# Graph network and mixture-of-experts kernel, one core: x plus normed x made in one ScalarE pass, GpSimd's bias add behind its gathers, x2 turned at the end of the outer layer, normalised rows ahead of the masks

## Chip, cores and metric

The kernel runs on one core of a Trainium2 chip. The metric is the time of one execution in device microseconds, the median of several runs.

## What is computed

6250 nodes with 256 features, 100000 edges with 96 features, sorted by target node. A graph network step comes first, then a mixture of 16 experts with two chosen per node. Both take layer-normalised rows and add their result to the rows they were given.

```python
# node network: edge_attr summed, maximised and averaged over each target node
out1 = segment_sum(edge_attr, col);  out2 = segment_max(edge_attr, col) or 0;  out3 = out1 / max(cnt, 1)
h = concatenate([x, out1, out2, out3, u[batch]], axis=1)
h = relu(h @ W1 + b1) @ W2 + b2
return h + x                                   # x here: the layer-normalised rows

# outer program
x = x + gnn(layernorm(x), ...)                 # so x1 = x + normed x + relu(...) @ W2 + b2
x = x + ffn(layernorm(x))                      # router, two of 16 experts, last layer norm
```

What matters here is x1 = (x + normed x + b2) + g, where g is the node network's output. Its first part, x + normed x + b2, is called RES in the kernel. x2 is the layer-normalised x1; its rows go to memory for the experts and, turned, to the router.

## The kernel before

All five engines are programmed by hand, each in its own block, and each runs its instructions in the order in which its code is written. They meet through counting semaphores.

**Edges.** VectorE scans ten chunks of edges backwards (running sum and running maximum of 96 features, 192 scans a chunk) and SP stores them. This runs until about 570 us, beside the node network.

**Node network.** It takes 25 macro tiles of 250 nodes, two sub-tiles of 125, from 122 to 771 us. Step i does:
- *TensorE* (`gnn_step`, L1088 on): first half of layer 1 (`layer1`, L1034 and L1036, closed by L1038), the router of two steps ago (`router`, L1067), second half of layer 1, the transposes of the next step's inputs (`turn`, L1015 and L1018), then layer 2 (`layer2`, L1048) in two halves, one for each sub-tile. Between these two, `between2` puts the transposes of x2 of the step before (`turn_x2`, L1060). The second half of layer 1 writes banks that ScalarE's first relu must have emptied.
- *ScalarE* (`gnn_step`, L877 on): store of x1, moments of the next x (`moments1`, L791 and L796), its share in the carry of the next macro tile (`carry_in`, L774 to L782), first relu (`relu`, L826), logits (L867), moments of x1 (`moments2`, L835 and L840), load of x two steps ahead (`load_x`, L800), then `mask_rows`: the masked edge results (L806 to L808) and the normalised node rows XN (L812). Then the second relu, `take_turned` (L817 to L819), x2 (`write_x2`, L848) and its store, `take_x2` (L863), and last `take_g` (L874), which copies g out of PSUM.
- *GpSimd* (`rows_step`): `add_rows` (L600), x1 = g + RES; `residual`, the next RES in two adds (L617 XN + x, L619 + b2); `cut` (L578); `norm1` (L591 to L595); `join` (L582 to L586); `norm2` (L605 to L610) of x1; and `gather` two steps ahead: an index copy (L563), a chain of branches on how many chunks must be in memory (L568), and six indirect DMAs (L571 to L573, twice), each issued by GpSimd itself.

`add_rows(i)` waits for g of step i and for RES of step i. Everything on ScalarE behind the store of x1 waits for `add_rows`.

```python
def residual(i, g, b):            # GpSimd
    pool.wait_ge(x1_ready, i)     # the RES before has been read
    pool.wait_ge(xr_got[b], ...); pool.wait_ge(node_rows, i + 1)
    RES = XN[b] + XR[b]           # L617
    RES = RES + b2bc              # L619
```

**Experts.** From 771 us TensorE runs 113 expert tiles (L1144, L1158, L1166) on rows that GpSimd gathers (L658) and scatters (L664). Its first instructions wait for the last-but-one macro tile's logits (L867). A last norm follows.

Of the kernel before, what the change touches and what calls it, by code (L numbers as in the profile page):

```python
# [28 lines left out]
P = 128  # L29
# [68 lines left out]
def after(i, g, b, n=1):  # L98

    return i + n, g + (b + n) // 2, (b + n) % 2  # L100


def gnn_moe_kernel(nc, x, dst, edge_attr, u, gW1, gb1, gW2, gb2, gate_w, gate_b,
# [83 lines left out]
    with ExitStack() as ctx:  # L187
        def sem(name):
            return ctx.enter_context(nc.semaphore(name))
# [32 lines left out]
        rowU = k.take(TILES, parts=NT, dt=U32)  # L222
        mean1, dev_1, rstd_1, nmr_1 = (k.take(2, parts=NT) for _ in range(4))
        Lo = k.take(TILES, NX, parts=NT)
# [144 lines left out]
        xr_got = [sem(f"xr_got{i}") for i in range(2)]  # L369
        residual_ready, x1_ready = sem("residual_ready"), sem("x1_ready")  # L370
        moments2_step, norm2_step, rstd2_ready = sem("moments2_step"), sem("norm2_step"), sem("norm2_rstd_ready")
# [146 lines left out]
        def _(pool):  # L518
# [68 lines left out]

            def norm1(i):
                s2 = Steps(pool, norm1_step, i * 2)
                hold(pool, moments1_step, i * 4 + 4)  # L590
                s2.mark(pool.tensor_scalar(dev_1, dev_1, 1.0 / D, EPS, ALU.mult, ALU.add))  # L591
                s2.wait()
                s2.mark(pool.tensor_tensor(rstd_1, dev_1, rpow, ALU.pow))
                s2.wait()
                pool.tensor_tensor(nmr_1, mean1, rstd_1, ALU.mult).then_inc(rstd1_ready, 1)  # L595

            def add_rows(i):
                pool.wait_ge(g_out, i + 2)
                pool.wait_ge(residual_ready, 2 * i + 2)
                pool.tensor_tensor(GO, GO, RES, ALU.add).then_inc(x1_ready, 1)  # L600
# [10 lines left out]

            def residual(i, g, b):
                if not isinstance(i, int) or i:
                    pool.wait_ge(x1_ready, i)
                pool.wait_ge(xr_got[b], (g + 1) * 16)
                pool.wait_ge(node_rows, i + 1)
                pool.tensor_tensor(RES, XN[b], XR[b][0:NT], ALU.add).then_inc(residual_ready, 1)  # L617
                pool.wait_ge(residual_ready, 2 * i + 1)
                pool.tensor_tensor(RES, RES, b2bc, ALU.add).then_inc(residual_ready, 1)  # L619

            def rows_step(i, g, b):
                more = not isinstance(i, int) or i + 1 < MACROS
                norm = not isinstance(i, int) or i >= 1
                if norm:
                    add_rows(i - 1)
                residual(i, g, b)
                if more:
                    cut(*after(i, g, b))
                    norm1(i + 1)
                    join(*after(i, g, b))  # L630
                if norm:
                    norm2(i - 1)
                if not isinstance(i, int) or i + 2 < MACROS:
                    gather(*after(i, g, b, 2))
            pool.sem_inc(joined, 1)
            gather(0, 0, 0)
            norm1(0)
            cut(0, 0, 0)
# [70 lines left out]
        def _(act):  # L709
# [91 lines left out]

            def mask_rows(i, g, b):
                act.wait_ge(joined, i + 2)
                for a in range(2):
                    j = bass.ds(2 * (MACROS - 1 - i) + a, 1)
                    act.activation(NB[b][:, a, 0:2 * EF], RAW[b][:, a, :, :].rearrange("p s f -> p (s f)"), ACT.Identity, scale=has[:, j])  # L806
                    act.activation(NB[b][:, a, 2 * EF:2 * P], RAW[b][:, a, 0, 0:EF - REST], ACT.Identity, scale=rch[:, j])
                    act.activation(NB[b][:, a, 2 * P:3 * P].rearrange("p (n r) -> p n r", n=QUAD), spread(RAW[b][:, a, 0, EF - REST:EF], 1, QUAD),  # L808
                                   ACT.Identity, scale=rch[:, j])
                act.wait_ge(rstd1_ready, i + 1)  # L810
                for a in range(2):
                    ins = act.activation(XN[b][:, a, :], XR[b][0:NT, a, :], ACT.Identity, bias=nmr_1[:, a:a + 1], scale=rstd_1[:, a:a + 1])  # L812
                ins.then_inc(node_rows, 1)

# [62 lines left out]
            def gnn_step(i, g, b, to=None):  # L877
# [13 lines left out]
                if norm:  # L891
                    moments2(i - 1, 0)
                    moments2(i - 1, 1)
                if not isinstance(i, int) or i + 2 < MACROS:
                    act.wait_ge(residual_ready, 2 * i + 2)
                    load_x(i + 2, b)
                if more:
                    mask_rows(*after(i, g, b))
                relu(i, 1)
                if more:  # L900
                    take_turned(*after(i, g, b))
                if norm:
                    write_x2(i - 1)
                    store_x2(i - 1, to)
                    take_x2(i - 1)
                take_g(i, g, b)
            moments1(0, 0, 0, 0)
# [75 lines left out]
        def _(pe):  # L983
# [104 lines left out]
            def gnn_step(i, g, b, amid1=None, behind1=None, amid2=None):  # L1088
# [5 lines left out]

                def between2():
                    if not isinstance(i, int) or i >= 1:
                        turn_x2(i - 1)
                    if amid2:
                        amid2()
                layer1(i, g, b, between1)  # L1100
                if behind1:
                    behind1()
                if not isinstance(i, int) or i + 1 < MACROS:
                    turn(*after(i, g, b))
                layer2(i, g, b, between2)
            turn(0, 0, 0)
# [522 lines left out]
```

## Time and profile before

| | |
|---|---|
| median of 3 runs | 1328.63 us (1326.2 to 1332.45) |
| the profiled execution: time | 1334.45 us |
| its span | 1332.7 us |
| granted TensorE clock, mean | 0.909 of full speed |
| node network | 122 to 771 us |
| experts | 771 to 1222 us |
| TensorE busy | 1185.9 us (89%) |
| GpSimd busy | 773.3 us (58%) |
| ScalarE busy | 646.1 us (48%) |
| VectorE busy | 788.0 us (59%) |

Times of the profile are microseconds from the span's start. A matmul of 32-bit numbers stands as two records, so a group of 800 is 400 matmuls. `PE` is TensorE, `PEld` its weight load, `DVE` VectorE, `ACT` ScalarE, `POOL` GpSimd; `ACTq` is an instruction of ScalarE's queue that is not counted as busy. In brackets stands how long the engine sat idle before the instruction and what ended it; "issue" is idle time for which the profile shows no releaser. A DMA issued by GpSimd occupies GpSimd for the time that it takes to write its descriptors, and that is what L571 to L573 show.

### The profile page before, as it was taken

To read this page: it belongs to the slowest core of one execution; us is meant where nothing else is said; L and a number is where in the kernel's file an instruction comes from. 1 tells how busy PE (TensorE), PEld (TensorE's weight loads), DVE (VectorE), ACT (ScalarE), POOL (GpSimd) and SP (SyncE) were. 2 spreads that over 40 slices of the span, in tenths; PEclk is the share of its full clock that TensorE was granted. 3 is DMA by queue.
4 is the path that set the end of the run, shared out by engine and by line. 5 is a ranking of instruction groups with operands and counts; after the bars stand their busy time and mean duration, and the time that the engine had idled before them with its cause. 6 is when DMAs were issued, how large, how long until landed. Compare 5 with 4: busy or idle time off the path is not lost.

```text
span 1332.7 us, 28448 instructions
## 1 busy us (share of the span) xinstructions
PE 1185.9 (89%) x6684; PEld 1003.7 (75%) x6685; DVE 788.0 (59%) x3039; ACT 646.1 (48%) x1969; POOL 773.3 (58%) x1061
## 2 busy tenths in 40 slices
PE   2003999999999999999999989999999999999798
PEld 1003888888888888878888888899999999997343
DVE  4999999899799899903534014542222222222886
ACT  5963556655665665655664332223333333333554
POOL 4876666666666667666754235556666666663222
PEclk7555999999999999989999989999999999998555
DMA  9986677768758775592110348856666666664763
GB/s 313 287 269 232 201 275 284 283 237 318 256 215 294 276 239 189 218 334 80 47 45 28 115 155 296 269 174 205 212 212 204 211 212 211 210 212 123 244 203 93
DMA packets 131029, 282.67 MB, mean 212 GB/s; under 512 B 25609, under 2 KB 38283, under 8 KB 130821
## 3 DMA queue, kind: packets, MB, share of 16 engines
q1 hardware_dynamic: 93937, 218.40, 48.3%
q0 software_dynamic: 26048, 43.47, 10.4%
q10 hardware_dynamic: 10964, 19.96, 4.4%
q8 instruction: 23, 0.38, 0.1%
q14 instruction: 57, 0.47, 0.1%
HBM read 167.27 MB, written 114.25 MB: 211 GB/s over the span
## 4 chain that ended last, share of the span: by engine, by line
PE 63%; DMA 10%; issue 9%; POOL 8%; ACT 7%; POOLq 2%; DVE 1%; ACTq 1%; SPq 0%; DVEq 0%
PE ps L1158 14%; PE ps L1166 13%; PE ps L1048 8%; PE ps L1034 7%; PE ps L1036 7%; DMA mem<-piece_carry,mem 4%; PE ps L1199 3%; PE ps L1201 3%; POOL mem L571 2%; POOL mem L572 2%; PE ps L1144 2%; DMA mem<-x_normed,mem 2%; DMA mem<-in_dst_dram,mem 2%; POOL mem L554 2%; ACT mem L728 1%
## 5 line engine op out<-in xcount | busy, mean ns | idle before, releaser
L924 ACT ACTIVATE mem<-ps,mem 128x128 f32<-128x128 f32 x452 | 128.9, 368 | 306.8 <-PE ps L1158 304.8
L1158 PEld LDWEIGHTS ps<-mem 128*128 128x128 f32 x1808 | 221.4, 194 | 7.9 <-issue 3.0
L1158 PE MATMUL ps<-mem 128*128 128x128 f32 x1808 | 223.9, 278 | 1.5 <-issue 1.5
L1034 PE MATMUL ps<-mem 128*128 128x250 f32 x800 | 208.5, 383 | 13.5 <-ACT mem L826 11.9
L1166 PE MATMUL ps<-mem 128*128 x904 | 215.7, 382 | 2.8 <-issue 2.6
L1253 DVE TENSOR_TENSOR_SCAN mem<-ps,mem 128x80 f32<-128x80 f32 x960 | 207.9, 297 | 0.3
L1257 DVE TENSOR_TENSOR_SCAN mem<-ps,mem 128x80 f32<-128x80 f32 x960 | 207.8, 302 | 0.0
L1036 PE MATMUL ps<-mem 128*128 128x250 f32 x800 | 204.4, 378 | 0.0
L664 POOL DMA_INDIRECT expert_rows<-mem x113 | 113.5, 1004 | 126.9 <-DVE mem L1515 112.6
L1048 PE MATMUL ps<-mem 128*125 128x256 f32 x800 | 181.0, 379 | 0.7 <-ACT mem L826 0.7
L1166 PEld LDWEIGHTS ps<-mem 128*128 128x128 f32 x904 | 163.5, 191 | 22.7 <-issue 4.9
L1034 PEld LDWEIGHTS ps<-mem 128*128 128x128 f32 x800 | 152.7, 194 | 33.2 <-ACT mem L826 14.2
L1036 PEld LDWEIGHTS ps<-mem 128*128 128x128 f32 x800 | 153.8, 192 | 18.6
L1048 PEld LDWEIGHTS ps<-mem 128*125 128x125 f32 x800 | 146.3, 188 | 21.1 <-ACT mem L826 1.1
L1508 DVE COPY mem<-ps 128x256 f32<-128x256 f32 x113 | 47.8, 424 | 178.2 <-PE ps L1144 175.9
L1515 DVE TENSOR_TENSOR mem<-ps,mem 128x256 f32<-128x256 f32 x113 | 47.9, 424 | 171.1 <-PE ps L1166 160.3
L658 POOL DMA_INDIRECT mem<-x_normed,mem x113 | 112.7, 998 | 35.4 <-issue 13.0
L1015 PE MATMUL ps<-mem 125*128 125x125 f32 x100 | 20.6, 288 | 90.5 <-ACT mem L812 90.5
L826 ACT ACTIVATE mem<-ps,mem 128x250 f32<-128x250 f32 x200 | 77.0, 467 | 48.6 <-PE ps L1038 48.6
L571 POOL DMA_INDIRECT mem<-run_max,mem x50 | 63.6, 1272 | 46.5 <-issue 46.5
L1015 PEld LDWEIGHTS ps<-mem 125*128 125x128 f32 x100 | 11.6, 145 | 97.7 <-issue 97.7
L554 POOL DMA_INDIRECT mem<-in_dst_dram,mem x50 | 62.1, 1241 | 29.7 <-ACT mem L745 14.7
(252 smaller groups left out, 1696.1 us busy)
## 6 DMA issues: line engine op xcount, KB each, us to landing
mem<-in_L_ffn_w_dram SPq DMA_DIRECT2D x129, 512.0 KB, 9.4
run_sum<-mem SPq DMA_DIRECT2D x80, 480.0 KB
run_max<-mem SPq DMA_DIRECT2D x80, 480.0 KB
mem<-in_edge_attr_dram SPq DMA_DIRECT2D x72, 480.0 KB, 8.0
mem<-expert_rows SPq DMA_DIRECT2D x22, 512.0 KB, 5.4
x_rows<-mem ACTq DMA_DIRECT2D x25, 256.0 KB, 4.0
x_normed<-mem ACTq DMA_DIRECT2D x25, 256.0 KB
mem<-in_x_dram ACTq DMA_DIRECT2D x24, 256.0 KB, 4.1
```

What stands on the lines that cost most here:

```text
L554: pool.indirect_dma_start(out=SR[:, slot % RING, :], out_offset=None, in_=dst2, in_offset=bass.IndirectOffsetOnAxis(rowU[:, j:j + 1], 0)). ...
L571: pool.indirect_dma_start(out=GM[b][:, a, :], out_offset=None, in_=s_max[0:edges], in_offset=last).then_inc(gathered[b], 16)
L658: pool.indirect_dma_start(out=XG[b], out_offset=None, in_=x2_d[0:rows], in_offset=bass.IndirectOffsetOnAxis(slot_now[b], 0)).then_inc(xg_g ...
L664: pool.indirect_dma_start(out=ya_d, out_offset=bass.IndirectOffsetOnAxis(into_now[b], 0), in_=YO[b], in_offset=None).then_inc(yo_stored[b] ...
L924: ins = act.activation(hT[b][:, c, :], bank(2 + b, c * P, (c + 1) * P), ACT.Relu, bias=eb1c[:, bass.ds(e, 1), c])
L1034: pe.matmul(h, W1x[:, c, hc * P:(hc + 1) * P], XT[b][:, c, :], start=(c == 0), stop=False)
L1036: pe.matmul(h, W1a[:, s, hc * P:(hc + 1) * P], AT[b][:, s, :], start=False, stop=False)
L1048: ins = pe.matmul(bank(5, a * D, (a + 1) * D, NT), H[:, hc, a * NT:(a + 1) * NT], W2[:, hc, :], start=(hc == 0), stop=(hc == HC - 1))
L1158: ins = pe.matmul(bank(2 + b, f * P, (f + 1) * P), w1now[q][:, c, f * P:(f + 1) * P], XgT[b][:, c, :], start=(c == 0), stop=(c == DC - 1))
L1166: ins = pe.matmul(bank(6 + b, 0, D), hT[b][:, c, :], w(c * D, D), start=(c == 0), stop=(c == FC - 1))
L1253: ins = dve.tensor_tensor_scan(out=Sb[:, ::-1, f], data0=keep[b][:, ::-1], data1=Eb[b][:, ::-1, f], initial=0.0, op0=ALU.mult, op1=ALU.add)
L1257: ins = dve.tensor_tensor_scan(out=Eb[b][:, ::-1, f], data0=bound[b][:, ::-1], data1=Eb[b][:, ::-1, f], initial=-FMAX, op0=ALU.min, op1=AL ...
```

## The change

- ScalarE makes RES's first part itself. x + normed x is x times (1 + rstd) plus the shift, one activation for each sub-tile (`twice`), so XN and x need not be added. GpSimd's L617 goes. For this GpSimd keeps 1 + rstd as well (`twice_1`), one more tiny operation, and the norm's values are double buffered.
- GpSimd's `residual` is only the b2 add, and it moves from behind `add_rows` to the end of `rows_step`, behind the gathers.
- On ScalarE, XN is made ahead of the masks and no longer behind them; the load of x moves behind the second relu; `take_x2` moves behind `take_g`.
- On TensorE, x2 is turned after both halves of layer 2, not between them.

```diff
@@ GpSimd @@
-            def norm1(i):
+            def norm1(i, b):
...
-                s2.mark(pool.tensor_tensor(rstd_1, dev_1, rpow, ALU.pow))
+                s2.mark(pool.tensor_tensor(rstd_1[:, b], dev_1, rpow, ALU.pow))
                 s2.wait()
-                pool.tensor_tensor(nmr_1, mean1, rstd_1, ALU.mult).then_inc(rstd1_ready, 1)
+                pool.tensor_tensor(shift_1[:, b], mean1, rstd_1[:, b], ALU.mult)
+                pool.tensor_scalar(twice_1[:, b], rstd_1[:, b], 1.0, None, ALU.add).then_inc(rstd1_ready, 1)
 
             def add_rows(i):
                 pool.wait_ge(g_out, i + 2)
-                pool.wait_ge(residual_ready, 2 * i + 2)
+                pool.wait_ge(residual_ready, i + 1)
                 pool.tensor_tensor(GO, GO, RES, ALU.add).then_inc(x1_ready, 1)
...
-            def residual(i, g, b):
-                if not isinstance(i, int) or i:
-                    pool.wait_ge(x1_ready, i)
-                pool.wait_ge(xr_got[b], (g + 1) * 16)
-                pool.wait_ge(node_rows, i + 1)
-                pool.tensor_tensor(RES, XN[b], XR[b][0:NT], ALU.add).then_inc(residual_ready, 1)
-                pool.wait_ge(residual_ready, 2 * i + 1)
+            def residual(i):
+                pool.wait_ge(twice_rows, i + 1)
                 pool.tensor_tensor(RES, RES, b2bc, ALU.add).then_inc(residual_ready, 1)
...
                 if norm:
                     add_rows(i - 1)
-                residual(i, g, b)
                 if more:
                     cut(*after(i, g, b))
-                    norm1(i + 1)
+                    norm1(i + 1, 1 - b)
                     join(*after(i, g, b))
                 if norm:
                     norm2(i - 1)
                 if not isinstance(i, int) or i + 2 < MACROS:
                     gather(*after(i, g, b, 2))
+                residual(i)
@@ ScalarE @@
             def mask_rows(i, g, b):
+                act.wait_ge(rstd1_ready, i + 1)
+                for a in range(2):
+                    act.activation(XN[b][:, a, :], XR[b][0:NT, a, :], ACT.Identity, bias=shift_1[:, b, a:a + 1], scale=rstd_1[:, b, a:a + 1])
                 act.wait_ge(joined, i + 2)
...
-                act.wait_ge(rstd1_ready, i + 1)
-                for a in range(2):
-                    ins = act.activation(XN[b][:, a, :], XR[b][0:NT, a, :], ACT.Identity, bias=nmr_1[:, a:a + 1], scale=rstd_1[:, a:a + 1])
...
+            def twice(i, b):
+                if not isinstance(i, int) or i:
+                    act.wait_ge(x1_ready, i)
+                for a in range(2):
+                    ins = act.activation(RES[:, a, :], XR[b][0:NT, a, :], ACT.Identity, bias=shift_1[:, b, a:a + 1], scale=twice_1[:, b, a:a + 1])
+                ins.then_inc(twice_rows, 1)
...
-                if not isinstance(i, int) or i + 2 < MACROS:
-                    act.wait_ge(residual_ready, 2 * i + 2)
-                    load_x(i + 2, b)
+                twice(i, b)
                 if more:
                     mask_rows(*after(i, g, b))
                 relu(i, 1)
+                if not isinstance(i, int) or i + 2 < MACROS:
+                    act.wait_ge(twice_rows, i + 1)
+                    load_x(i + 2, b)
                 if more:
                     take_turned(*after(i, g, b))
                 if norm:
                     write_x2(i - 1)
                     store_x2(i - 1, to)
+                take_g(i, g, b)
+                if norm:
                     take_x2(i - 1)
-                take_g(i, g, b)
@@ TensorE @@
-                def between2():
-                    if not isinstance(i, int) or i >= 1:
-                        turn_x2(i - 1)
-                    if amid2:
-                        amid2()
...
-                layer2(i, g, b, between2)
+                layer2(i, g, b, amid2)
+                if not isinstance(i, int) or i >= 1:
+                    turn_x2(i - 1)
```

Where the instructions stand. GpSimd, a step in the middle of the stage, from the last gather to the next macro tile's join. Before:

```order
L573 DMA mem<-piece_carry,mem 125x192
L568 UNCONDITIONAL_BRANCH
L600 TENSOR_TENSOR mem<-mem 125x512
L617 TENSOR_TENSOR mem<-mem 125x512
L619 TENSOR_TENSOR mem<-mem 125x512
L578 TENSOR_TENSOR mem<-mem 125x192
L591 TENSOR_SCALAR mem<-mem 125x2
L593 TENSOR_TENSOR mem<-mem 125x2
L595 TENSOR_TENSOR mem<-mem 125x2
L582 TENSOR_TENSOR mem<-mem 125x2x96
```

Now (L616 is the b2 add, L602 the add that makes x1, L597 the 1 + rstd):

```order
L574 DMA mem<-piece_carry,mem 125x192
L569 UNCONDITIONAL_BRANCH
L616 TENSOR_TENSOR mem<-mem 125x512
L602 TENSOR_TENSOR mem<-mem 125x512
L579 TENSOR_TENSOR mem<-mem 125x192
L592 TENSOR_SCALAR mem<-mem 125x2
L594 TENSOR_TENSOR mem<-mem 125x2
L596 TENSOR_TENSOR mem<-mem 125x2
L597 TENSOR_SCALAR mem<-mem 125x2
L583 TENSOR_TENSOR mem<-mem 125x2x96
```

One add of 125x512 is gone from behind the add that makes x1, and the other now stands between the last gather and it.

ScalarE, from the second moments of x1 to the second relu. Before:

```order
L840 ACTIVATE mem<-mem 125x256 x2
L800 DMA mem<-in_x_dram 128x512
L806 ACTIVATE mem<-mem 125x192
L807 ACTIVATE mem<-mem 125x64
L808 ACTIVATE mem<-mem 125x128
L806 ACTIVATE mem<-mem 125x192
L807 ACTIVATE mem<-mem 125x64
L808 ACTIVATE mem<-mem 125x128
L812 ACTIVATE mem<-mem 125x256 x2
L826 ACTIVATE mem<-ps,mem 128x250 x4
```

Now (L844 the moments, L816 RES, L802 XN, L830 the relu):

```order
L844 ACTIVATE mem<-mem 125x256 x2
L816 ACTIVATE mem<-mem 125x256 x2
L802 ACTIVATE mem<-mem 125x256 x2
L806 ACTIVATE mem<-mem 125x192
L807 ACTIVATE mem<-mem 125x64
L808 ACTIVATE mem<-mem 125x128
L806 ACTIVATE mem<-mem 125x192
L807 ACTIVATE mem<-mem 125x64
L808 ACTIVATE mem<-mem 125x128
L830 ACTIVATE mem<-ps,mem 128x250 x4
L797 DMA mem<-in_x_dram 128x512
```

Two passes of 125x256 have come in ahead of the masks, XN's two have moved ahead of them too, and the load of x stands behind the relu.

TensorE at the end of the stage, from layer 2 of the last step to the experts. Before:

```order
L1048 MATMUL ps<-mem 125x256 x8
L1060 MATMUL ps<-mem 128x125 x4
L1048 MATMUL ps<-mem 125x256 x8
L1067 MATMUL ps<-mem 125x16 x4
L1144 MATMUL ps<-mem 128x128 x4
L1158 MATMUL ps<-mem 128x128 x16
```

Now (L1066 turns x2, L1073 is the router, L1147 and L1161 the experts):

```order
L1044 MATMUL ps<-mem 128x250 x4
L1054 MATMUL ps<-mem 125x256 x16
L1066 MATMUL ps<-mem 128x125 x4
L1073 MATMUL ps<-mem 125x16 x4
L1147 MATMUL ps<-mem 128x128 x4
L1161 MATMUL ps<-mem 128x128 x16
```

The transposes of x2 now stand right ahead of the router that needs them, through ScalarE's copy.

## Rows read from the trace of the kernel before

**Rows 1.** The page: busy time of each engine (1), loads of node rows (6).
```profile
PE 1185.9 (89%) x6684; PEld 1003.7 (75%) x6685; DVE 788.0 (59%) x3039; ACT 646.1 (48%) x1969; POOL 773.3 (58%) x1061
...
mem<-in_x_dram ACTq DMA_DIRECT2D x24, 256.0 KB, 4.1
```

**Rows 2.** GpSimd's groups, 155 to 700 us: instruction, count, busy us, mean ns, idle before.
```profile
L617 POOL TENSOR_TENSOR mem<-mem 125x512 f32<-125x512 f32 x21 | 27.6, 1317 | 3.2 <-POOL mem L600 2.4
...
L619 POOL TENSOR_TENSOR mem<-mem 125x512 f32<-125x512 f32 x21 | 22.9, 1091 | 1.6
...
L563 POOL COPY mem<-mem 125x4 uint32 (+1 forms) x22 | 4.4, 202 | 25.8 <-issue 25.8
...
L605 POOL TENSOR_SCALAR mem<-mem 125x2 f32<-125x2 f32 x22 | 4.4, 199 | 34.4 <-ACT mem L840 34.4
```

**Rows 3.** Who waited for whom, 155 to 700 us: total us, times, longest us.
```profile
POOL mem L600 <- ACT mem L874: 11.9, 13, 2.8
...
PE ps L1034 <- ACT mem L826: 11.3, 14, 2.7
...
ACT mem L774 <- DMA mem<-piece_carry,mem: 10.8, 8, 2.1
```

**Rows 4.** One round in order of time: start us, us, engine, line, operation, idle before.
```profile
525.90 1.01 PE L1034 MATMUL ps<-mem 128*128 128x250 f32 x4
...
527.83 1.29 POOL L600 TENSOR_TENSOR mem<-mem 125x512 f32<-125x512 f32 x1
...
532.53 0.64 ACT L774 ACTIVATE mem<-mem 125x96 f32<-125x96 f32 x2 [0.30 <-ACT mem L796]
...
535.00 1.11 PE L1034 MATMUL ps<-mem 128*128 128x250 f32 x4 [0.56 <-ACT mem L826]
...
538.51 0.19 POOL L605 TENSOR_SCALAR mem<-mem 125x2 f32<-125x2 f32 x1 [1.47 <-ACT mem L840]
...
539.23 0.46 ACT L806 ACTIVATE mem<-mem 125x192 f32<-125x192 f32 x1 [0.92 <-ACT mem L840]
...
541.00 1.07 ACT L812 ACTIVATE mem<-mem 125x256 f32<-125x256 f32 x2
...
541.96 0.70 PE L1038 MATMUL ps<-mem 32*128 32x250 f32 x8
...
551.05 1.01 PE L1034 MATMUL ps<-mem 128*128 128x250 f32 x4
...
551.35 0.66 ACT L874 ACTIVATE mem<-ps 125x256 f32<-125x256 f32 x2 [2.97 <-PE ps L1048]
551.48 1.21 POOL L573 DMA_INDIRECT mem<-piece_carry,mem  x1 [0.30 <-issue]
552.72 1.28 POOL L600 TENSOR_TENSOR mem<-mem 125x512 f32<-125x512 f32 x1
```

**Rows 5.** TensorE behind two long waits; last row a stretch: length, busy, clock, DMA share, GB/s.
```profile
309.30 1.96 PE L1034 MATMUL ps<-mem 128*128 128x250 f32 x4 [1.59 <-ACT mem L826]
...
317.93 0.49 PE L1038 MATMUL ps<-mem 32*128 32x250 f32 x4
...
587.07 2.03 PE L1034 MATMUL ps<-mem 128*128 128x250 f32 x4 [2.69 <-ACT mem L826]
...
596.79 0.70 PE L1038 MATMUL ps<-mem 32*128 32x250 f32 x8
...
587.00:597.00 10.00, 9.93 (x36) 0.71 1.10 351
```

**Rows 6.** The end of the stage, in order of time.
```profile
767.51 0.59 ACT L863 ACTIVATE mem<-ps 128x500 f32<-128x500 f32 x1 [2.19 <-PE ps L1060]
...
770.76 0.94 PE L1067 MATMUL ps<-mem 128*125 128x16 f32 x8
770.96 0.66 ACT L874 ACTIVATE mem<-ps 125x256 f32<-125x256 f32 x2 [2.87 <-PE ps L1048]
```

**Rows 7.** The first step, in order of time.
```profile
131.13 0.64 ACT L774 ACTIVATE mem<-mem 125x96 f32<-125x96 f32 x2 [6.35 <-DMA mem<-piece_carry,mem]
```

More of the change, by code:

```diff
@@ L222, in gnn_moe_kernel @@
         rowU = k.take(TILES, parts=NT, dt=U32)
-        mean1, dev_1, rstd_1, nmr_1 = (k.take(2, parts=NT) for _ in range(4))
+        mean1, dev_1 = (k.take(2, parts=NT) for _ in range(2))
+        rstd_1, twice_1, shift_1 = (k.take(2, 2, parts=NT) for _ in range(3))
         Lo = k.take(TILES, NX, parts=NT)
@@ L369, in gnn_moe_kernel @@
         xr_got = [sem(f"xr_got{i}") for i in range(2)]
-        residual_ready, x1_ready = sem("residual_ready"), sem("x1_ready")
+        twice_rows, residual_ready, x1_ready = sem("x_and_normed_x"), sem("residual_ready"), sem("x1_ready")
         moments2_step, norm2_step, rstd2_ready = sem("moments2_step"), sem("norm2_step"), sem("norm2_rstd_ready")
@@ L634, in rows_step @@
                     gather(*after(i, g, b, 2))
+                residual(i)
             pool.sem_inc(joined, 1)
             gather(0, 0, 0)
-            norm1(0)
+            norm1(0, 0)
             cut(0, 0, 0)
@@ L807, in mask_rows @@
                     act.activation(NB[b][:, a, 2 * EF:2 * P], RAW[b][:, a, 0, 0:EF - REST], ACT.Identity, scale=rch[:, j])
-                    act.activation(NB[b][:, a, 2 * P:3 * P].rearrange("p (n r) -> p n r", n=QUAD), spread(RAW[b][:, a, 0, EF - REST:EF], 1, QUAD),
-                                   ACT.Identity, scale=rch[:, j])
-                act.wait_ge(rstd1_ready, i + 1)
+                    ins = act.activation(NB[b][:, a, 2 * P:3 * P].rearrange("p (n r) -> p n r", n=QUAD), spread(RAW[b][:, a, 0, EF - REST:EF], 1, QUAD),
+                                         ACT.Identity, scale=rch[:, j])
+                ins.then_inc(node_rows, 1)
+            def twice(i, b):
+                if not isinstance(i, int) or i:
+                    act.wait_ge(x1_ready, i)
                 for a in range(2):
-                    ins = act.activation(XN[b][:, a, :], XR[b][0:NT, a, :], ACT.Identity, bias=nmr_1[:, a:a + 1], scale=rstd_1[:, a:a + 1])
-                ins.then_inc(node_rows, 1)
+                    ins = act.activation(RES[:, a, :], XR[b][0:NT, a, :], ACT.Identity, bias=shift_1[:, b, a:a + 1], scale=twice_1[:, b, a:a + 1])
+                ins.then_inc(twice_rows, 1)
             def take_turned(i, g, b):
```

## Prediction

> **What bounds the kernel now.** I read the page first. TensorE is busy for 89% of the span [rows 1], so at first sight it is the bound, and what can be won or lost is the time in which it waits. The stage that the change touches runs from 122 to 771 us: 25 macro tiles through the node network. I took the stretch 155 to 700 us, where the loop is regular, and asked first for GpSimd's groups [rows 2], then for who waits for whom [rows 3], then for one round in order of time [rows 4].
>
> The reader should see three things. First, TensorE waits in one place, the second half of layer 1 (L1034), for ScalarE's first relu (L826): 11.3 us in all [rows 3]. Second, ScalarE is late there because x1 came late: GpSimd's add (L600) frees the two moment passes and the carry, and the relu queues behind those. Third, GpSimd's add is late mostly because of GpSimd itself. In [rows 4] its last gather instruction starts at 551.48 and takes 1.21, until 552.69, and L600 starts at 552.72, while ScalarE had handed over g at 551.35 + 0.66 = 552.01. In the whole stretch L600 waited for ScalarE's g in 13 of 21 rounds, 11.9 us in all [rows 2, 3].
>
> So there is a closed round that TensorE is not part of: L600 (527.83), the carry on ScalarE (L774, 532.53), first relu, second moments, GpSimd's norm (L605, 538.51, after 1.47 us of idleness), index copy, six gather issues (the last from 551.48), L600 again (552.72): 24.89 us. TensorE's own step goes from 525.90 to 551.05, 25.15 us, 0.56 of them waiting: 24.59 us of work [rows 4]. **The round of GpSimd and ScalarE and that of TensorE are within 0.3 us of each other, and here the first is the longer.** What is put into the first is paid for.
>
> **GpSimd's first add goes (L617).** It costs 1.32 us a round [rows 2], but lies behind L600 and ahead of the cut. The instruction that closes GpSimd's free section, L605, waits for ScalarE's moments: 34.4 us in 22 rounds [rows 2]. What is taken out ahead of L605 only makes that idle time longer, from 1.6 us on average to about 2.8. The cut (L578) comes earlier too, but ScalarE's carry waited for its own moment passes (L774 at 532.53, released by L796) and not for GpSimd, so nothing starts sooner. Worth 0. If that cover were gone it would be worth at most 21 x 1.32 = 27.7.
>
> **The bias add moves behind the gathers (L619).** Here it stands between the last gather and L600, inside the round. Each of the 21 rounds of the stretch gets 22.9 / 21 = 1.09 us and 1.6 / 21 = 0.08 of idleness [rows 2]: 21 x 1.17 = 24.6 us. Two things take it up. The first is the 11.9 us in which L600 waited for g: slack of GpSimd, all of which can be used up (at the least 9: the longest wait, 2.8 us, gives only 1.17, and two more may be like it). And the gathers' landings: in 8 rounds the carry L774 waits for them, 10.8 us in all [rows 3]. They land at the same distance from their issue, so a later L600 waits less for them. Each absorbs 1.17 less what L600 had waited: 8 x 1.17 = 9.4 at most, 0 at least, and I take the middle, 5. Net 24.6 - 11.9 - 5 = **+7.7 us**.
>
> **Slow halves.** Longer rounds mean longer TensorE waits. After a wait of 1.59 us the second half of layer 1 took 317.93 - 309.30 = 8.63 us, after 2.69 us it took 596.79 - 587.07 = 9.72, against 541.96 - 535.00 = 6.96 after 0.56 [rows 4, 5]; the granted clock was 0.71 in the slow stretch, that is a mix of 1.2 and 2.4 GHz. TensorE's waits should grow from 11.3 to about 20 us, some 8 of them over 1.5 us. A slow half costs 1.7 to 2.8, but TensorE's side then has room: in [rows 4] g would be ready 0.5 us ahead of GpSimd, with the bias add 1.17 more, with x2's transposes out of the middle another 0.4. About 0.3 us leaks from each: **+2.5**, with 0 and 8 x 1.0 = 8 as ends. The Trainium skill (TensorE: Matmul & The Clock Gate, What's actually happening) has the array's clock fall to half after idle time; by it every long wait might be followed by a slow half, which is the third rival below.
>
> **ScalarE's two passes more (RES from x).** No row has them; the nearest is L812, the same shape, 1.07 for a pair [rows 4]. They stand after the second moments and ahead of XN and the masks. Today XN ends at 541.00 + 1.07 = 542.07. Ahead of the masks ScalarE stood 0.92 us, in which the x load was issued (L806); take that out, put 1.07 in, and the rows are ready at about 542.2, while TensorE asks for them at 541.96 + 0.70 = 542.66 [rows 4]. It just fits; 0.3 late would still lie in TensorE's new slack. Taken at 0, ends 0 and 21 x 0.3 = 6, the latter hidden by the same slack. XN ahead of the masks costs nothing: rstd comes long before. GpSimd's small extra add, 125x2 like L605 (0.19), ends before the carry's result is due: 0.
>
> **The x load behind the second relu.** It is issued some 6 us later than today, about 17 us into the round, and lands in 4.1 [rows 1]; its first reader is a moment pass some 2 us into the next round. That leaves 5 us: 0, unless landings double.
>
> **x2 turned after layer 2.** In the rounds TensorE does the same work in another order, and g comes 0.4 sooner, which is used above. At the handover it costs: today the router (L1067) follows layer 2 at once, at 770.76 [rows 6]. Now it needs transposes, g taken first (0.20 + 0.66), then x2 taken (0.59), some 0.15 of signalling: 1.6, less about 0.4 for the four transposes that leave layer 2 (estimated from the router's 0.94 for eight matmuls). **+1.2**, between 0.6 and 1.8.
>
> **Start.** XN ahead of the masks frees 1.08 us before the first transposes, but the first relu waits for gathers that land at 131.13 whatever ScalarE did [rows 7]: 0.
>
> **Sum.** 7.7 + 2.5 + 1.2 = +11.4 us. The profiled execution took 1334.45 us, so 1345.9; it stands 5.8 us above the median of the runs, 1328.63. Against the median: **1340.0 us**, 0.9% slower. With the ends: least 24.6 - 11.9 - 9.4 + 0 + 0.6 = +3.9, most 24.6 - 9 - 0 + 8 + 1.8 = +25.4, and as these are hardly at their ends together, about +20.
>
> **Rivals.**
> - *Faster: the work taken off GpSimd shortens the round.* It would hold if the section ahead of L605 bound it, so that cut, carry and relu all came earlier. TensorE's 11.3 us of waits and the two slow halves (1.7 + 2.8) go, the handover stays: -14.6, 1314.0 us. Against it stand 34.4 us of idleness ahead of L605. It decides from where that idleness is 0. The Trainium skill says to prefer other engines to GpSimd where possible (Perfetto Trace Analysis, Optimizing GPSIMD Operations); by that rule the swap of a GpSimd add for ScalarE passes is this gain. Chance 0.08.
> - *No change: GpSimd's issue time shrinks.* 25.8 us ahead of L563 are "issue", idle time without a releaser [rows 2]. If an emptier queue took 0.5 us from each round, 21 x 0.5 = 10.5 would cancel all but 0.9 of the loss: 1329.5. For it, only that this row is unexplained; against it, that the queue already stood idle. Chance 0.12.
> - *Worse: slow halves in full.* Eight at 2.25 with nothing absorbed, less the 4.5 of today: 7.7 + 1.2 + 18 - 4.5 = +22.4, 1351.0 us. Chance 0.10.
> - The order of instructions shows that the change does what it says.
>
> **Numbers.** The forecast has 0.70; about 0.08 of it lies under +6.6 us, which is 0.5% and about what a measurement of this kernel can tell. So slower 0.62 + 0.10 = 0.72, same 0.08 + 0.12 = 0.20, faster 0.08. The range 1331 to 1350 leaves out the faster rival and most of the worse one, and holds the upper half of the no-change case.
>
> **What would show it.** In the changed profile: the bias add starting within 0.1 us of the last gather's end and L600's counterpart right behind it, in nearly all rounds; idleness before L605's counterpart of 1.6 us or more; TensorE's waits at the second half near 20 us; the round of [rows 4] near 25.5 us or above; the router 1.6 us behind layer 2 at the handover. Wrong, if GpSimd sits idle between its last gather and the bias add or the add of g, if TensorE's waits fall, or if TensorE starts to wait at the transposes of the node rows.

## The result and the profile after

The changed kernel takes 1339.58 us in the median of 4 runs (1339.05 to 1340.1), against 1328.6 (1326.2 to 1332.45) for the kernel before, run beside it: ratio 1.008, 95% interval 1.0055 to 1.0104. The forecast of 1340.0 us, slower, held. A ratio here leaves out the executions more than 1.5% above the fastest of their kernel, so it is not always that of the two medians.

The profiled execution of the changed kernel took 1339.05 us, 0.5 below its median; that of before stands 5.8 above its own. So the two traces differ by 4.6 us only, and most of the excess of before lies in a stage that the change does not touch: from the first expert transposes to the last stage it took 450.2 us, and 445.5 in a second trace of the same kernel (below). I compare the node network alone, and give both traces of before.

| | before | before, second trace | after |
|---|---|---|---|
| first x1 add to the 22nd | 533.98 us | 534.98 | 541.14 |
| mean of its last 20 rounds | 25.48 | 25.53 | 25.85 |
| last x1 add to first expert transposes | 0.59 | 0.59 | 2.09 |
| experts, to the start of the last stage | 450.23 | 445.50 | 448.25 |

The page of the changed kernel, its first busy line:

```profile
PE 1185.8 (89%) x6684; PEld 1003.7 (75%) x6685; DVE 790.2 (59%) x3039; ACT 668.5 (50%) x2019; POOL 749.6 (56%) x1061
```

TensorE's work is the same [rows 1]. GpSimd has 23.7 us less to do, ScalarE 22.4 more: the swap took place and did not pay. GpSimd's groups from 155 to 705 us (instruction, count, busy us, mean ns, idle before), which answer to [rows 2]. L602 makes x1, L616 is the bias add, L607 opens the second norm, L564 is the index copy:

```profile
L602 POOL TENSOR_TENSOR mem<-mem 125x512 f32<-125x512 f32 x21 | 27.6, 1313 | 3.9 <-POOL mem L616 1.4 <-ACT mem L878 1.0
L616 POOL TENSOR_TENSOR mem<-mem 125x512 f32<-125x512 f32 x21 | 23.2, 1103 | 0.6
...
L607 POOL TENSOR_SCALAR mem<-mem 125x2 f32<-125x2 f32 x22 | 5.0, 228 | 33.3 <-ACT mem L844 33.3
L564 POOL COPY mem<-mem 125x4 uint32 (+1 forms) x22 | 4.3, 197 | 22.2 <-issue 22.2
```

Ahead of the x1 add GpSimd hardly waits for g any more: 1.0 us, where it was 11.9 [rows 3]. The 34.4 us ahead of the second norm [rows 2] are 33.3. The two adds that stood ahead of the cut, 27.6 + 22.9 us [rows 2], left GpSimd idle one step earlier: ahead of the cut, 14.2 us before, 37.1 now, and ahead of the first norm, 0.6 before, 24.4 now. Who waited for whom in the same stretch (total us, times, longest):

```profile
POOL mem L579 <- DMA mem<-piece_carry,mem: 37.1, 14, 4.6
...
POOL mem L592 <- ACT mem L793: 24.4, 13, 2.7
...
PE ps L1040 <- ACT mem L830: 17.2, 17, 1.9
...
ACT mem L771 <- DMA mem<-piece_carry,mem: 5.1, 5, 1.5
```

TensorE's wait for the first relu rose from 11.3 us to 17.2, and the carry's wait for its gathers fell from 10.8 to 5.1 [rows 3]. In order of time (start us, us, engine, line, operation, idle before), two long waits, one round that answers to [rows 4], and the end of the stage, which answers to [rows 6]:

```profile
259.90 1.41 PE L1040 MATMUL ps<-mem 128*128 128x250 f32 x4 [1.85 <-ACT mem L830]
...
268.54 0.70 PE L1044 MATMUL ps<-mem 32*128 32x250 f32 x8
...
337.01 1.11 PE L1040 MATMUL ps<-mem 128*128 128x250 f32 x4 [1.70 <-ACT mem L830]
...
343.96 0.70 PE L1044 MATMUL ps<-mem 32*128 32x250 f32 x8
...
533.37 1.29 POOL L602 TENSOR_TENSOR mem<-mem 125x512 f32<-125x512 f32 x1
...
538.07 0.64 ACT L771 ACTIVATE mem<-mem 125x96 f32<-125x96 f32 x2 [0.30 <-ACT mem L793]
...
544.05 0.19 POOL L607 TENSOR_SCALAR mem<-mem 125x2 f32<-125x2 f32 x1 [1.47 <-ACT mem L844]
...
547.27 0.19 POOL L564 COPY mem<-mem 125x4 uint32 x1 [1.47 <-issue]
...
549.21 1.33 POOL L572 DMA_INDIRECT mem<-run_max,mem  x1 [1.75 <-issue]
...
549.77 0.43 PE L1021 MATMUL ps<-mem 125*128 125x125 f32 x2
...
556.91 1.21 POOL L574 DMA_INDIRECT mem<-piece_carry,mem  x1 [0.30 <-issue]
...
558.10 0.66 ACT L878 ACTIVATE mem<-ps 125x256 f32<-125x256 f32 x2 [4.37 <-issue]
558.14 1.11 POOL L616 TENSOR_TENSOR mem<-mem 125x512 f32<-125x512 f32 x1
...
559.40 1.28 POOL L602 TENSOR_TENSOR mem<-mem 125x512 f32<-125x512 f32 x1 [0.15 <-POOL mem L616]
...
776.90 0.59 ACT L867 ACTIVATE mem<-ps 128x500 f32<-128x500 f32 x1
777.10 1.26 POOL L602 TENSOR_TENSOR mem<-mem 125x512 f32<-125x512 f32 x1 [5.96 <-ACT mem L878]
777.55 1.04 PE L1073 MATMUL ps<-mem 128*125 128x16 f32 x8 [0.80 <-ACT mem L867]
...
779.19 0.90 PE L1147 MATMUL ps<-mem 128*128 128x128 f32 x4 [0.60 <-ACT mem L871]
```

In the round, the last gather ends at 556.91 + 1.21 = 558.12. The bias add follows at 558.14, the x1 add at 559.40, 1.28 us behind the last gather; g had been ready at 558.10 + 0.66 = 558.76. In the trace the same 1.28 or 1.29 us stand between the last gather and the x1 add in 19 of the 21 rounds. In the other two it is 1.52 and 1.77, because the x1 add waited for g there. The node rows' transposes (549.77) follow layer 1 without a wait: ScalarE's two passes more were in time. Two other gaps to remember are 1.47 us ahead of the index copy and 1.75 ahead of the first gather, both without a releaser.

### The profile page after: what moved, and what is told of

The parts are those of the page before. It is cut to its first block, busy times and chain, and to the rows that moved or that the text cites. A ratio compares the mean times of both kernels' runs of the same rounds, so it can differ in the third digit from the quotient of the medians.

```text
span 1337.3 us, 28483 instructions
## 1 busy us (share of the span) xinstructions
PE 1185.8 (89%) x6684; PEld 1003.7 (75%) x6685; DVE 790.2 (59%) x3039; ACT 668.5 (50%) x2019; POOL 749.6 (56%) x1061
## 4 chain that ended last, share of the span: by engine, by line
PE 58%; POOL 11%; issue 10%; DMA 8%; ACT 8%; POOLq 2%; ACTq 1%; DVE 1%; SPq 0%; DVEq 0%
PE ps L1161 14%; PE ps L1169 13%; PE ps L1040 6%; PE ps L1042 6%; PE ps L1054 6%; PE ps L1202 3%; PE ps L1204 3%; DMA mem<-in_dst_dram,mem 3%; DMA mem<-piece_carry,mem 3%; POOL mem L572 3%; POOL mem L573 2%; DMA mem<-x_normed,mem 2%; PE ps L1147 2%; ACT mem L830 2%; ACT mem L725 1%
## 5 line engine op out<-in xcount | busy, mean ns | idle before, releaser
L1161 PEld LDWEIGHTS ps<-mem 128*128 128x128 f32 x1808 | 220.8, 194 | 9.6 <-issue 4.4
L1161 PE MATMUL ps<-mem 128*128 128x128 f32 x1808 | 223.9, 278 | 2.1 <-issue 2.0
L1169 PEld LDWEIGHTS ps<-mem 128*128 128x128 f32 x904 | 163.4, 191 | 21.5 <-issue 3.5
L1054 PE MATMUL ps<-mem 128*125 128x256 f32 x800 | 177.7, 379 | 0.7 <-ACT mem L830 0.7
L830 ACT ACTIVATE mem<-ps,mem 128x250 f32<-128x250 f32 x200 | 77.2, 468 | 41.3 <-PE ps L1044 41.2
```

What stands on the lines that cost most here:

```text
L830: act.activation(H[:, hc, :], bank(H_BANKS[q][hc - q * QUAD], 0, M), ACT.Relu, bias=cbias[:, hc:hc + 1]).then_inc(h_ready, 1)
L1054: ins = pe.matmul(bank(5, a * D, (a + 1) * D, NT), H[:, hc, a * NT:(a + 1) * NT], W2[:, hc, :], start=(hc == 0), stop=(hc == HC - 1))
L1161: ins = pe.matmul(bank(2 + b, f * P, (f + 1) * P), w1now[q][:, c, f * P:(f + 1) * P], XgT[b][:, c, :], start=(c == 0), stop=(c == DC - 1))
L1169: ins = pe.matmul(bank(6 + b, 0, D), hT[b][:, c, :], w(c * D, D), start=(c == 0), stop=(c == FC - 1))
```

## Experiments

All ran beside the kernel before, whose median was 1331.87 us in one group (both adds back, the bias add alone, no bias add, both adds back with the copy ahead) and 1331.95 in the other (the other two with the copy ahead, x2 in the middle, the bias add twice). The changed kernel was not run again in either. A difference between medians of two groups is therefore weaker than one inside a group. The two runs made for second traces had a run of before beside them that took 1347.22. The expectations speak of the round of GpSimd and ScalarE from the prediction: from one x1 add to the next. A slow half is a second half of layer 1 that takes 8.3 us or more where the others take 6.9 to 7.0.

**Both adds back where they were.** From the changed kernel: the two GpSimd adds return behind the x1 add (`residual` is (XN + x) + b2, as before), ScalarE's passes for RES go. What is left of the change is x2's place, XN ahead of the masks and the later load of x.

```diff
@@ GpSimd, from the changed kernel @@
...
                     add_rows(i - 1)
+                residual(i, g, b)
...
-                residual(i)
@@ ScalarE @@
-                twice(i, b)
```

> The changed kernel with both adds of GpSimd back behind the add that makes x1, and ScalarE's two passes gone; XN ahead of the masks, the late load of x and x2 turned behind layer 2 all stay. Theory (the bias add sits in the round of GpSimd and ScalarE): the 21 x 1.17 us leave the round, the handover's 1.2 us stay: 1329 to 1331 us, L600's counterpart again waits for g in about half of the rounds. Rival (the order of x2, of the x load or of XN costs the time): it stays at 1337 us or more.

Measured: 1334.19 us (12 runs), ratio 1.0013 (0.9987 to 1.004). The 22 adds span 533.73 us (before 533.98 and 534.98), TensorE waits 11.1, and the handover takes 2.09 us, as after. So these three parts cost 1.5 us at the handover and nothing in the rounds. The median lies above the 1329 to 1331 us that were expected, but these were counted from a median of 1328.6 for the kernel before, and here that one stood at 1331.87.

**No bias add at all.** From the changed kernel: ScalarE's passes stay, `residual` goes.

```diff
             def add_rows(i):
...
-                pool.wait_ge(residual_ready, i + 1)
+                pool.wait_ge(twice_rows, i + 1)
...
-                residual(i)
```

> The changed kernel without any b2 add (b2 of the node network is left out). Theory: only the 1.17 us of each round go, and the round is as before: 1328 to 1331 us. Rival (ScalarE's two passes delay the node rows or the relu): 1334 us or more, and TensorE waits ahead of the transposes of the node rows (L1021).

Measured: 1330.03 us (12 runs), ratio 0.9994 (0.9978 to 1.001). GpSimd had both adds less than in the kernel before, 2.4 us a round, and the time was that of before. The waits of its trace show where the free time goes:

```profile
POOL mem L579 <- DMA mem<-piece_carry,mem: 50.9, 20, 6.5
...
POOL mem L607 <- ACT mem L840: 37.8, 22, 2.6
```

50.9 us at the cut and 37.8 at the second norm: GpSimd comes early to work that ScalarE and the gathers hold back. This answers the faster rival: less work on GpSimd ahead of the second norm brought nothing. (ScalarE's two passes stayed, so a small gain that they cancel is not excluded; no run took the adds away without them.) From here to the changed kernel the only step is one add of 1.1 us behind the gathers. The medians are 1330.03 and 1339.58, from different groups; in the traces 5.5 us of it stand between the first and the 22nd x1 add (535.60 to 541.14).

**The bias add alone behind the gathers,** from the kernel before; L617 stays. ScalarE is as it was, but for its load of x, which now waits for the first add only.

```diff
+            def bias(i):
                 pool.wait_ge(residual_ready, 2 * i + 1)
                 pool.tensor_tensor(RES, RES, b2bc, ALU.add).then_inc(residual_ready, 1)
...
                     gather(*after(i, g, b, 2))
+                bias(i)
...
-                    act.wait_ge(residual_ready, 2 * i + 2)
+                    act.wait_ge(residual_ready, 2 * i + 1)
```

> The kernel before with one thing changed: the b2 add goes behind the gathers, the add of XN and x stays where it was. Theory: the whole loss of the rounds comes with this alone, 7.7 + 2.5 us, without the handover's 1.2: 1337 to 1340 us, the bias add back to back with the last gather in nearly all rounds. Rival (two passes on ScalarE or x2's place cost the time): within 2 us of 1328.6.

Measured: 1338.12 us (9 runs), ratio 1.006 (1.0033 to 1.0086): most or all of the loss of the change, by this one line's place. With the two above, the parts are separated: the bias add's place alone loses; without it the times are within 0.2% of the kernel before. Its profiled execution took 1362.22 us, far above that median, so I ran it once more, and the kernel before as well.

> The kernel before once more, for a second trace: the executions of it spread over 1326 to 1335 us, and its first profile lies at the upper end. Expected: rounds of 25.2 to 25.6 us, and the difference between the two traces outside the rounds, in the first gathers' landings and in the expert stage, by up to 6 us.

> e2_bias_alone once more, since its profile fell on a disturbed execution. Theory: rounds of 25.8 to 26.1 us, the bias add 1.28 us ahead of L600 throughout, the handover at 0.6 us: 1335 to 1341 us. Rival (the bias add alone costs less than the whole change): rounds under 25.6 us.

The kernel before gave 1330.41 us, with the numbers in the table above. The other missed its expectation: 1355.58 us, one run, beside that run of before of 1347.22. Its rounds are 26.65 us (26.64 in the first trace), 1.1 to 1.2 above before. Two places differ. The gap ahead of the index copy sums to 33.7 us (33.0 in the first trace), where before has 25.8 and 25.5. And there are 8 slow halves (7 in the first trace), where before has 2 and 3; behind five of them the x1 add waited for g, up to 2.40 us. Neither trace is of an execution near the median, so where the 6 to 8 us (by the medians, by the ratio) went in this kernel is not shown by a trace.

**The bias add twice.** If the round of GpSimd and ScalarE is closed, a second add there must be paid in full, since the slack was used up by the first. From the changed kernel; b2 is then added twice.

```diff
             def add_rows(i):
...
-                pool.wait_ge(residual_ready, i + 1)
+                pool.wait_ge(residual_ready, 2 * i + 2)
...
                 pool.tensor_tensor(RES, RES, b2bc, ALU.add).then_inc(residual_ready, 1)
+                pool.wait_ge(residual_ready, 2 * i + 1)
+                pool.tensor_tensor(RES, RES, b2bc, ALU.add).then_inc(residual_ready, 1)
```

> The changed kernel with the b2 add issued twice behind the gathers (so b2 is added twice). Theory: GpSimd has next to no idle time left ahead of the add that makes x1 (2.4 us in 21 rounds), and only the waits for late gathers, 5 us, can still give way: 21 x 1.17 = 24.6, less 2 to 5, plus one or two slow halves: 1359 to 1366 us. Rival (most of the first add's price was something else, such as late gathers): the second costs no more than the first, under 1352 us.

Measured: 1358.87 us (6 runs), ratio 1.0213 (1.0181 to 1.0244), at the lower edge of the 1359 to 1366 that were expected. One round's end, in order of time:

```profile
549.97 1.22 POOL L574 DMA_INDIRECT mem<-piece_carry,mem  x1 [0.31 <-issue]
551.21 1.11 POOL L616 TENSOR_TENSOR mem<-mem 125x512 f32<-125x512 f32 x1
552.40 1.09 POOL L618 TENSOR_TENSOR mem<-mem 125x512 f32<-125x512 f32 x1
553.57 1.28 POOL L602 TENSOR_TENSOR mem<-mem 125x512 f32<-125x512 f32 x1
```

The second add puts 552.40 - 551.21 = 1.19 us into a round, and the mean round is 27.00 instead of 25.85: 1.15. The first add cost 0.26 (25.59 without it, 25.85), the second all of it. This kernel has 8 slow halves and 28.4 us of TensorE waits, and still its rounds grew by no more than the add. Behind only one of the 8 did the x1 add wait for g, 0.81 us: with two adds in GpSimd's round, what TensorE loses in a slow half is nearly all hidden beside it.

**x2 in the middle of layer 2 again,** from the changed kernel, and taken ahead of g.

```diff
@@ ScalarE @@
                     store_x2(i - 1, to)
+                    take_x2(i - 1)
                 take_g(i, g, b)
-                if norm:
-                    take_x2(i - 1)
@@ TensorE @@
-                layer2(i, g, b, amid2)
-                if not isinstance(i, int) or i >= 1:
-                    turn_x2(i - 1)
+                def between2():
+                    if not isinstance(i, int) or i >= 1:
+                        turn_x2(i - 1)
+                    if amid2:
+                        amid2()
+                layer2(i, g, b, between2)
```

> The changed kernel with x2 turned between the two halves of layer 2 again and taken ahead of g. Theory: rounds as in the changed kernel, since GpSimd closes them 1 to 2 us behind g; the handover falls from 2.1 to 0.6 us: 1337 to 1340 us. Rival (the earlier g matters): slower than the changed kernel, 1341 us or more.

Measured: 1337.07 us (12 runs), ratio 1.0055 (1.0025 to 1.0084), beside 1.008 for the change; the intervals overlap. The handover is back at 0.60 us, so its 1.5 us are shown by the trace, not by the medians. The runs spread widely (1330.54 to 1348.39), and the profiled one, 1344.41, lies in their upper part: its rounds of 26.33 us are no measure of the median's. The bias add alone, which also has the bias add behind the gathers and x2 in the middle of layer 2, spreads widely too (1333.81 to 1362.22), while the four runs of the changed kernel lie within 1.1 us. The three traces of this combination have 7, 8 and 7 slow halves, that of the changed kernel 3. Whether x2's place keeps the changed kernel steady was not tested.

**The index copy ahead of the second norm.** In all kernels so far GpSimd goes through second norm, gap, index copy, gap, first gather. If this round sets the time, taking one gap into the idleness ahead of the second norm must win. The same edit was made in three kernels: in that with both adds back, in the changed one, and in the one before.

```diff
@@ GpSimd @@
-            def gather(i, g, b):
+            def index_copy(i, g, b):
...
+                return level
+
+            def gather(i, g, b, level=None):
+                if level is None:
+                    level = index_copy(i, g, b)
...
+                ahead = not isinstance(i, int) or i + 2 < MACROS
+                if ahead:
+                    level = index_copy(*after(i, g, b, 2))
                 if norm:
                     norm2(i - 1)
-                if not isinstance(i, int) or i + 2 < MACROS:
-                    gather(*after(i, g, b, 2))
+                if ahead:
+                    gather(*after(i, g, b, 2), level)
```

> As e1_adds_back, and GpSimd's index copy with its load of the level stands ahead of the norm of x1, in the idle time that GpSimd has there. Theory (the round binds): the copy's 0.2 us and the 0.9 to 1.6 us of idleness ahead of it leave the round, TensorE's own step of 24.4 us binds, its waits fall from 11 us to under 4 and the slow halves go: 1316 to 1321 us. Rival (the issue time ahead of the copy is instruction handling that comes back ahead of the first gather, or TensorE's step is the bound already): within 3 us of e1_adds_back.

> The changed kernel as it is, with the bias add behind the gathers, and only the index copy and the load of the level ahead of the norm of x1. In e4_copy_ahead GpSimd then stood 31 us ahead of 21 adds, 1.5 us a round. Theory (what counts is which round is longer): the bias add's 1.17 us now fit into that idle time and cost nothing: 1311 to 1316 us, as e4_copy_ahead. Rival (the bias add costs its 1.17 us wherever GpSimd is in sequence): about 1322 us or more.

> The kernel before with the index copy and the load of the level ahead of the norm of x1, nothing else. Theory: TensorE's own step binds as in e4_copy_ahead and the handover is the short one: 1309 to 1314 us, about 1.5 us under e4_copy_ahead, the candidate for the fastest. Rival (x2 behind layer 2 helps the rounds by handing g over 0.4 us sooner): 1315 us or more, and TensorE waits again for the first relu.

| the copy moved in | runs | median us | ratio to before | round | TensorE waits |
|---|---|---|---|---|---|
| both adds back | 6 | 1312.72 | 0.9874 (0.9841 to 0.9906) | 24.62 | 0.7 |
| the changed kernel | 6 | 1314.58 | 0.9897 (0.9865 to 0.9929) | 24.70 | 1.9 |
| the kernel before | 5 | 1311.30 | 0.9855 (0.9832 to 0.9877) | 24.64 | 0.9 |

The last has the lowest median here, though its interval overlaps those of the other two; all three beat the kernel before and the changed one. One round of it, GpSimd in order of time (L563 the copy, L610 to L615 the second norm, L576 the first gather, L605 the x1 add):

```profile
539.20 1.28 POOL L605 TENSOR_TENSOR mem<-mem 125x512 f32<-125x512 f32 x1 [1.53 <-ACT mem L882]
...
549.40 0.19 POOL L563 COPY mem<-mem 125x4 uint32 x1 [1.09 <-issue]
549.81 0.19 POOL L610 TENSOR_SCALAR mem<-mem 125x2 f32<-125x2 f32 x1 [0.22 <-ACT mem L848]
...
551.36 0.19 POOL L615 TENSOR_TENSOR mem<-mem 125x2 f32 x1 [0.27 <-POOL mem L613]
553.17 1.33 POOL L576 DMA_INDIRECT mem<-run_max,mem  x1 [1.62 <-issue]
```

From the norm's end to the first gather it is 553.17 - 551.55 = 1.62 us. In the kernel with both adds back and the copy behind the norm, the same stretch reads:

```profile
542.36 0.19 POOL L612 TENSOR_TENSOR mem<-mem 125x2 f32 x1 [0.28 <-POOL mem L610]
543.99 0.19 POOL L564 COPY mem<-mem 125x4 uint32 x1 [1.44 <-issue]
545.93 1.33 POOL L572 DMA_INDIRECT mem<-run_max,mem  x1 [1.75 <-issue]
```

545.93 - 542.55 = 3.38 us: the edit takes 1.76 us out of the round. The copy's gap lies beside ScalarE's moments now and did not come back ahead of the first gather. The first of the three came out below the 1316 to 1321 us expected of it, the other two inside their ranges. Now GpSimd waits for g again, and here stands the same bias add in a round that is open. The row of the x1 add, 155 to 705 us, first in the changed kernel with the copy ahead:

```profile
L607 POOL TENSOR_TENSOR mem<-mem 125x512 f32<-125x512 f32 x22 | 28.8, 1309 | 13.7 <-ACT mem L886 12.3 <-POOL mem L621 0.6
```

and in the kernel before with the copy ahead:

```profile
L605 POOL TENSOR_TENSOR mem<-mem 125x512 f32<-125x512 f32 x22 | 28.8, 1309 | 47.5 <-ACT mem L882 47.5
```

The waits for g fall from 47.5 to 12.3 us. The kernel with both adds back and the copy ahead lies between, with 39.2: that is 8.3 us or 0.4 a round less than in the kernel before with the copy ahead, which fits g coming sooner once x2's transposes have left the middle of layer 2. The other 26.9 us, 1.22 for each of 22 rounds, are the bias add, inside waiting time. Now compare two pairs that differ by the same step, from both adds back to the changed order. With the copy behind the norm the 22 x1 adds span 533.73 and 541.14 us, with the copy ahead 516.28 and 517.92. **The same step costs 7.4 us of the rounds where GpSimd's round sets the time, and 1.6 where TensorE's does.** The medians say the same less sharply, 1334.19 to 1339.58 and 1312.72 to 1314.58, since each of these pairs spans two groups of runs. Inside one group, the changed kernel and the kernel before, both with the copy ahead, are 3.3 us apart, with intervals that overlap, and the handover explains 1.5.

## Why the prediction was right

*The closed round* was right, and it carries the result. The trace shows the bias add within 0.1 us of the last gather in all 21 rounds and the x1 add right behind; two adds cost the second in full; 1.76 us taken out elsewhere in the round, until TensorE set its length, brought 21 to 25 us.

*The bias add, +7.7.* The stretch grew by 541.14 - 533.98 = 7.2 us against the profiled execution of before and by 6.2 against its second trace. Of its 24.6 us, 9.5 went into GpSimd's waits ahead of the x1 add (11.9 to 2.4; I had 11.9) and 5.7 into the carry's waits for the gathers (10.8 to 5.1; I had 5). That leaves 9.4, and 2.2 to 3.2 of it did not show up either. The gap ahead of the copy shrank from 25.8 us to 22.2, which would do, but the same row reads 21.5 with both adds back and 25.2 with the bias twice, so it is no effect of the bias add that I can name. This shrinking also hid a slip of mine. A wait of GpSimd can take up no more than the 1.17 us of the add, and the 11.9 us consist of 2.79, 2.19, 1.56 and 1.19 and nine shorter ones of 4.2 in all: usable were 4 x 1.17 + 4.2 = 8.8, below even the 9 that I had as the lower end. With 8.8 the same sum gives 24.6 - 8.8 - 5 = +10.8 in place of +7.7. That +7.7 came so close to the measured 6.2 to 7.2 is in part luck.

*Slow halves, +2.5: this term was mis-sized.* TensorE's waits are 17.2 us where I said 20, with 4 over 1.5 us (1.85, 1.70, 1.55, 1.92), not 8. Only 3 of all were followed by a slow half, as many as in the second trace of before, one more than in the first. What leaked from them can be read at the x1 add, which waits for g if TensorE is late. First the adds behind the two slow halves of before, then those behind the first two of the changed kernel; behind its third there was no wait for g:

```profile
328.18 1.28 POOL L600 TENSOR_TENSOR mem<-mem 125x512 f32<-125x512 f32 x1 [2.19 <-ACT mem L874]
...
606.92 1.26 POOL L600 TENSOR_TENSOR mem<-mem 125x512 f32<-125x512 f32 x1 [2.79 <-ACT mem L874]
...
200.44 1.28 POOL L602 TENSOR_TENSOR mem<-mem 125x512 f32<-125x512 f32 x1 [0.39 <-ACT mem L878]
...
278.25 1.28 POOL L602 TENSOR_TENSOR mem<-mem 125x512 f32<-125x512 f32 x1 [0.64 <-ACT mem L878]
```

So the 0.3 us of leak that I took for each is about right in the changed kernel (1.0 us for three), and the count was wrong. Before, the x1 add waited 2.2 and 2.8 us behind the two slow halves, the TensorE waits ahead of them included: without the bias add in its way GpSimd reached the x1 add earlier there and stood idle for longer. The term should have been 1 us at most, inside its ends of 0 and 8.

*The handover, +1.2:* 2.09 - 0.59 = 1.5, inside 0.6 to 1.8. It is x2's transposes, 0.59 us, the router's wait of 0.80 for their copy (777.55), and a router 0.1 longer. The experts' transposes wait 0.60 for the logits (779.19), but so they did before:

```profile
772.30 0.63 PE L1144 MATMUL ps<-mem 128*128 128x128 f32 x4 [0.60 <-ACT mem L867]
```

*ScalarE's passes, the load of x, L617, each 0:* the kernel with both adds back and the one without the bias add lie within 0.2% of before, and between them they contain all these parts. ScalarE's masks started at 545.88, 1.83 us behind L607, where they were 0.72 behind before [rows 4] (539.23 - 538.51), as the two passes made them, and TensorE did not wait for the rows. But the forecast was wrong about where L617's time would turn up: not as longer idleness ahead of the second norm (34.4 to 33.3, or 1.5 a round, where I had it grow from 1.6 to about 2.8) but ahead of the cut and the first norm, since the join behind them starts when ScalarE's carry is ready, no sooner than today.

*The start, 0:* the first x1 add came at 149.19 us, 1.2 earlier than in the trace of before; over the traces of this study it lies between 147.9 and 154.9 us. The two latest, 153.6 and 154.9, are those of the bias add alone; the others show no order by kernel.

*The sum* was +11.4. The traces give 6.2 to 7.2 in the rounds and 1.5 at the handover, less 0.6 in the three rounds between the 22nd x1 add and the last (87.33 us before, 86.77 after), 7.1 to 8.1 in all; the medians give 11.0, with an interval from 7.3 to 13.8. So the forecast met the median closely, in part because the term for the slow halves stood in for something that the traces don't show. The 2.9 to 3.9 us between traces and medians I assign to nothing. The 11.0 rest on four runs of each kernel; the kernel before had a median of 1328.6 us in these and of 1331.9 in the 42 beside the experiments.

*The rivals.* Faster: fell, by the kernel with no bias add, and by its own sign: the idleness ahead of L605's counterpart is 33.3 us and not 0. The Trainium skill's advice to prefer other engines to GpSimd (Perfetto Trace Analysis, Optimizing GPSIMD Operations) brought nothing here: 23.7 us went from GpSimd to ScalarE, and no time with them. No change by less issue time: the gap ahead of the copy fell by 3.6 us, not by 10.5. Worse by slow halves in full: fell, with 3 of them.

## What to carry to other kernels

An engine at 58% of the span can still close a round: follow one round from an instruction to itself, and compare its length with the busiest engine's. Slack taken by the first microsecond put into such a round is gone for the second, so ask for each edit how much of the round's waits is left. And idle time without a releaser inside the round can be worth more than a faster instruction beside it: here, putting a tiny copy ahead of a wait that was there anyway gave 21 to 25 us against the same kernel without it, more than all parts of the change cost together.

## What was not expected of the hardware

The wait's length does not tell whether a slow half follows. After the two waits shown above the second half of layer 1 took 268.54 - 259.90 = 8.64 us and 343.96 - 337.01 = 6.95. Stretches of the changed kernel (length, busy of each engine, granted clock, DMA share, GB/s):

```profile
260.00:270.00 10.00, 10.00 (x48) 8.20 (x49) 10.00 (x48) 7.57 (x24) 5.27 (x10) 0.83 0.15 58
337.00:347.00 10.00, 9.99 (x56) 8.54 (x57) 9.42 (x37) 9.24 (x28) 5.02 (x10) 1.00 0.47 178
```

The first stretch has a granted clock of 0.83, a mix of 1.2 and 2.4 GHz, the second the full 2.4, after 1.85 and 1.70 us of waiting. In the changed kernel a wait of 1.07 us (at 182 us) was followed by 8.60 us, one of 1.92 (at 593) by 6.96. In the trace of before the slow halves came after waits of 1.59 and 2.69 and not after 1.38, which had looked like a threshold. In the twelve traces together, 252 of these second halves lie between the first and the 22nd x1 add. The 45 slow halves among them followed waits of 0.94 to 3.82 us. No slow half followed a shorter wait, but 21 waits above 0.94, up to 2.40, were followed by none. What decides it stays open.

The gap ahead of GpSimd's index copy, 1.47 us in the round shown, shrinks to 1.09 or 0.70 when the copy moves to another place, and its sum over the stretch differs from kernel to kernel, with nothing in the trace that releases it. With the copy in its old place it is 25.5 to 33.7 us in the four traces of kernels built on the one before, and 21.5 to 25.7 in the five built on the changed one. I had treated it as a fixed price; it is the largest thing in this round whose cause I can't name.
